# The setup of a graph layer's kernel in another order: list and first gathers before x, tables of chunk 0 before the lead groups

## The chip, the cores and the metric

The kernel runs on one core of a Trainium2 chip. The metric is the time of one execution on the device in microseconds (us), lower is better. The engines have short names in the profile: PE (TensorE, matmuls), PEld (its weight loads), DVE (VectorE), ACT (ScalarE), POOL (GpSimd) and SP (SyncE, which here only issues transfers); a q behind a name is that engine's instruction queue.

## The reference, cut to what matters

```python
def _L0_gnn_ref(x, edge_index, edge_attr, W1, b1, W2, b2, ln_w, ln_b, gn_w, gn_b, gn_ms):
    src, dst = (edge_index[0], edge_index[1])
    msg = x[src] + edge_attr
    agg = jax.ops.segment_sum(msg, dst, num_segments=N)
    h = jax.nn.relu(agg @ W1 + b1) @ W2 + b2
    ...   # a norm over all of h, a graph norm, gelu, + x
x = _layernorm(x + _L0_gnn_ref(x, edge_index, edge_attr_128, ...), axis=-1)
```

There are N = 6250 nodes with 128 features and E = 206250 edges, sorted by their target dst. For each node the kernel sums the 128 features of every incoming edge (edge_attr) and the features x of every edge's source node.

## The kernel before, in words

The aggregate agg (128 features x 6250 nodes, in SBUF) has two parts, and one long loop builds both.

*The edge part.* The edges are cut into 68 groups of 3072, and a group comes in two halves of 768 KB each, `edges`, in a ring of four slots (`HALVES = 4`). VectorE makes a one-hot matrix per half (`mark`, L1029), TensorE multiplies (`sum_half`, L722), ScalarE copies the sums (`copy_sums`, L573), TensorE puts them in place with a one-hot `place` (`turn_sums`, L736), and VectorE adds them to agg (`add`, L1053). The first four groups are the lead groups (`lead_groups`, `mark_lead`), halves 0 to 7; the rest run inside the chunk loop. A half's load waits until the half that had its slot has been read (semaphore `halves_free`); halves 8 to 12, which chunk 0 reads, wait for half 6, for half 7 (halves 9, 10 and 11) and for half 8.

*The source part.* The nodes are cut into 25 chunks of 250, that is 125 pairs. For each chunk TensorE counts how often each source node occurs: VectorE marks five batches (`mark_batch`, L1118, two bf16 comparisons each), TensorE counts 25 banks (`count_bank`, L774, 5 matmuls each), ScalarE copies each bank (`copy_bank`, L609), and then x is multiplied with the counts (L832, 98 matmuls, x split in two fp32r parts `x_hi` and `x_lo`). Banks 0 to 5 of a chunk are counted ahead, among the products of the chunk before. Chunk 0 has no chunk before it.

*What a chunk's marks need.* Each edge is one word with dst and src; the words are stored to a list in DRAM (`listed`). To find a pair's edges, two gathers by GpSimd follow each other for each chunk c: `begins(c)` (L479) reads 256 words around the pair's tile, VectorE counts the words below the pair and so finds the row (`stage_row`, L1076 to L1080), and `near(c)` (L486) reads the 128 words from there. VectorE splits the words (`split_words`, `widen_words`, `join_keys`, L1089 to L1103), TensorE turns them (`turn_keys`, L751), ScalarE copies them (`copy_keys`, L579), and the marks can start. `begins(c+1)` waits for `stage_tile(c+1)`, which stands behind `join_keys(c)` on VectorE. So the gathers of chunks 0, 1 and 2 are a chain through GpSimd, the DMA engines and VectorE.

*The setup.* SP loads dst, ACT loads src; VectorE packs the words (L982), ACT stores the list. A search finds for each pair the tile of 256 edges: three pieces, 7 sets each, marked by VectorE (piece 0, L962) or ScalarE (pieces 1 and 2, L553) and summed by TensorE (L694). In the kernel before, SP loads x as soon as src has landed, into the memory of the marks (`x_raw` in `pool_m`), so no mark can be written until x has been split. SP's queue is in order: dst, x, then the edge halves.

The order on each engine is written out by hand. The profile's lines are those of the functions below.

## Time and profile before

| | us |
|---|---|
| time, median of 3 runs (753.02 to 753.58) | 753.34 |
| the profiled execution | 756.05 |
| its span in the profile | 754.2 |

| engine | busy us | share of the span |
|---|---|---|
| PE | 691.8 | 92% |
| PEld | 628.4 | 83% |
| DVE | 631.5 | 84% |
| ACT | 424.5 | 56% |
| POOL | 115.1 | 15% |

The profiled execution takes 756.05 us, 1.85 us more than its span. The mean granted clock of TensorE is 0.974 of full speed. The page's first part gives busy time by engine; its second part cuts the span in 40 slices; its fourth part follows the work that ended last back from the end. A stretch can be asked for alone: the chain of waits in order of time, a timeline of instructions, or busy time by windows. Idle time of an engine matters only where somebody waits for it.

### The profile page before, as it was taken

What the parts mean: (1) busy time and instruction counts of PE and PEld (TensorE: products, weight loads), DVE (VectorE), ACT (ScalarE), POOL (GpSimd) and SP (SyncE); (2) the same over time, 40 slices, a digit from 0 to 9 for tenths busy, and PEclk for the clock granted to TensorE, in tenths of its full rate; (3) what the DMA queues carried; (4) which work ended last, traced back from release to release, by engine and by line L of the source; (5) the groups of instructions that cost most, each with busy time, mean ns of one, the idle gap of its engine ahead of it and who ended that gap; (6) DMA issues with size and microseconds to landing.
All of it is one profiled execution on the core that took longest, in us unless ns stands there. A gap on an engine that the chain in (4) does not pass through costs nothing.

```text
span 754.2 us, 25355 instructions
## 1 busy us (share of the span) xinstructions
PE 691.8 (92%) x9473; PEld 628.4 (83%) x9473; DVE 631.5 (84%) x1067; ACT 424.5 (56%) x962; POOL 115.1 (15%) x90
## 2 busy tenths in 40 slices
PE   0976899999999999999999999999999999999963
PEld 0965789988899888998899988999889998888842
DVE  4786989889899898998989989899898998835576
ACT  0943565466655666457564566646665466614447
POOL 2042301110011101111011110211101110100024
PEclk9995799999999999999999999999999999999996
DMA  6957535466354662556625665356553565400006
GB/s 136 329 191 220 182 99 198 152 219 209 88 190 170 214 209 71 196 185 212 196 74 187 206 208 172 100 179 217 189 172 119 177 219 172 144 16 0 0 1 170
DMA packets 87489, 120.41 MB, mean 160 GB/s; under 512 B 8718, under 2 KB 84486, under 8 KB 87267
## 3 DMA queue, kind: packets, MB, share of 16 engines
q1 hardware_dynamic: 80724, 113.10, 46.6%
q0 software_dynamic: 5744, 5.38, 2.7%
q10 hardware_dynamic: 1000, 1.65, 0.9%
q8 instruction: 13, 0.21, 0.1%
q14 instruction: 8, 0.07, 0.0%
HBM read 116.03 MB, written 4.03 MB: 159 GB/s over the span
## 4 chain that ended last, share of the span: by engine, by line
PE 76%; ACT 9%; DVE 5%; DMA 4%; issue 3%; POOL 1%; ACTq 0%; DVEq 0%; POOLq 0%; SPq 0%
PE bank L832 40%; PE bank L774 18%; PE bank L722 10%; ACT counts L609 6%; PE bank L876 3%; PE bank L866 3%; PE bank L736 2%; ACT below L553 2%; DMA begins<-listed,tile_slot 2%; DMA agg<-in_dst_dram 1%; DMA near<-listed,row_slot 1%; POOL pool_m L526 1%; DVE x_lo L1059 1%; PE bank L751 1%; DVE pool_m L1118 1%
## 5 line engine op out<-in xcount | busy, mean ns | idle before, releaser
L609 ACT CAST counts<-bank 128x490 fp32r<-128x490 f32 x600 | 320.1, 605 | 239.0 <-PE bank L774 236.1
L832 PE MATMUL bank<-counts,x_hi 128*128 128x250 f32 x1225 | 308.7, 291 | 8.5 <-ACT counts L609 8.4
L832 PE MATMUL bank<-counts,x_lo 128*128 128x250 f32 x1225 | 293.2, 279 | 0.0
L832 PEld LDWEIGHTS bank<-counts,x_hi 128*128 128x128 f32 x1225 | 231.1, 189 | 14.8 <-ACT counts L609 14.0
L1118 DVE TENSOR_TENSOR pool_m<-value_row,turned_lo 128x3328 bf16<-128x3328 bf16 (+1 forms) x125 | 229.1, 1833 | 12.1 <-PE bank L774 11.6
L832 PEld LDWEIGHTS bank<-counts,x_lo 128*128 128x128 f32 x1225 | 232.3, 190 | 0.0
L774 PE MATMUL bank<-pool_m 128*128 128x98 bf16 x3125 | 196.0, 211 | 8.6 <-DVE pool_m L1118 8.6
L774 PEld LDWEIGHTS bank<-pool_m 128*128 128x128 bf16 x3125 | 159.6, 99 | 28.3 <-issue 12.8
L1118 DVE TENSOR_TENSOR pool_m<-value_row,turned_key 128x2548 bf16<-128x2548 bf16 (+1 forms) x125 | 179.7, 1437 | 0.0
L486 POOL DMA_INDIRECT near<-listed,row_slot x27 | 53.6, 1986 | 501.6 <-DVE row_slot L1080 460.0
L722 PE MATMUL bank<-edges,onehot 128*32 128x128 f32 x3228 | 121.6, 284 | 5.9 <-DMA edges<-in_edge_attr_dram 3.9
L722 PEld LDWEIGHTS bank<-edges,onehot 128*32 128x32 f32 x3228 | 84.3, 112 | 18.6 <-issue 3.9
L1029 DVE TENSOR_TENSOR onehot<-value_row,dst_cols 128x384 f32<-128x384 bf16 x136 | 72.8, 553 | 0.0
L1053 DVE TENSOR_TENSOR agg<-agg,bank 128x128 f32 x68 | 19.4, 285 | 29.4 <-PE bank L736 27.9
L479 POOL DMA_INDIRECT begins<-listed,tile_slot x28 | 37.1, 1326 | 40.5 <-issue 29.7
L654 ACT ACTIVATE onehot<-bank,b1c 128x250 f32<-128x250 f32 x50 | 20.7, 465 | 27.3 <-PE bank L866 27.3
L573 ACT COPY sums<-bank 128x128 f32<-128x128 f32 x68 | 21.5, 316 | 22.3 <-PE bank L722 22.2
L736 PE MATMUL bank<-place,sums 128*128 128x128 f32 x136 | 32.3, 320 | 0.7 <-DVE place L1041 0.5
L736 PEld LDWEIGHTS bank<-place,sums 128*128 128x128 f32 x136 | 20.7, 191 | 11.8 <-issue 8.3
L1126 DVE CAST counts<-bank 128x490 fp32r<-128x490 f32 x25 | 16.6, 665 | 13.0 <-PE bank L774 13.0
L1331 DVE TENSOR_SCALAR agg<-bank,par 128x250 f32 x24 | 11.5, 478 | 17.3 <-PE bank L876 17.3
L866 PE MATMUL bank<-agg,pool_m 128*128 (+1 forms) x100 | 25.1, 374 | 0.8 <-DVEq L1315 0.8
(156 smaller groups left out, 461.7 us busy)
## 6 DMA issues: line engine op xcount, KB each, us to landing
edges<-in_edge_attr_dram SPq DMA_DIRECT2D x134, 768.0 KB
out_dram<-pool_m SPq DMA_DIRECT2D x12, 256.0 KB
agg<-in_dst_dram SPq DMA_DIRECT2D x1, 768.0 KB
agg<-in_src_dram ACTq DMA_DIRECT2D x1, 768.0 KB
listed<-agg ACTq DMA_DIRECT2D x1, 768.0 KB
begins<-listed,tile_slot POOLq DMA_INDIRECT x28, 4.2
near<-listed,row_slot POOLq DMA_INDIRECT x27
pool_m<-in_L_gnn_W_dram SPq DMA_DIRECT2D x2, 128.0 KB, 2.2
```

The lines of the kernel that those rows point to most:

```text
L479: pool.indirect_dma_start(begins[0:PAIRS, :], None, listed_rows, bass.IndirectOffsetOnAxis(tile_slot[0:PAIRS, 0:1], 0)).then_inc(begins_lo ...
L486: pool.indirect_dma_start(near[0:PAIRS, :], None, listed_rows, bass.IndirectOffsetOnAxis(row_slot[0:PAIRS, 0:1], 0)).then_inc(near_loaded, 16)
L573: nc.scalar.copy(sums[:, :], eps[s]).then_inc(sums_copied, 1)
L609: nc.scalar.copy(counts[:, :, at:at + NODES], cps[k % RING][:, 0:NODES * NT].rearrange("p (n q) -> p q n", q=NT)).then_inc(banks_free, 1)
L722: last = nc.tensor.matmul(eps[s][b * WINDOW:(b + 1) * WINDOW, :], oh[:, t, :], edges[:, u, t * D:(t + 1) * D], start=(k == 0 and j == 0), ...
L736: nc.tensor.matmul(turned_sum[s], sums[:, :], place[:, :], start=True, stop=True).then_inc(sums_turned, 1)
L774: last = nc.tensor.matmul(cps[k % RING][:, i * KEYS:(i + 1) * KEYS], mark_lo[b % MARKED][:, n // INTER, :, n % INTER], mark_key[b % MARKED ...
L832: last = nc.tensor.matmul(sps[:, 0:CHUNK], part[:, q, :], counts[:, q, at:at + CHUNK], start=(q == 0 and part is x_hi), stop=(q == NT - 1 ...
L866: last = nc.tensor.matmul(zps[u][:, k, 0:CHUNK], w1[:, k * P:(k + 1) * P], agg[:, bass.ds(c * CHUNK, CHUNK)], start=True, stop=True, skip_ ...
L876: last = nc.tensor.matmul(hps[u][:, 0:CHUNK], w2[:, k, :], hidden[:, u, k, :], start=(k == 0), stop=(k == HC - 1))
L1029: dve.tensor_tensor(oh, window, of.to_broadcast([P, HALF, WINDOW]), ALU.is_equal).then_inc(onehot_ready, 1)
L1118: last = dve.tensor_tensor(to[b % MARKED][:, 0:wide[1]], values[:, :, 0:n, :].to_broadcast(wide), of.to_broadcast(wide), ALU.is_equal)
```

## The change

Four things are put elsewhere; nothing is computed otherwise.

1. The small loads of dst and src (the last 3 full rows and the rest) are issued ahead of the large ones (64 rows). The padding of the last row no longer is a memset in the target: VectorE sets one row (`pad_row`), and GpSimd copies it with a DMA.
2. x is loaded into the place of `x_lo` (`x_in`) and split in place, so the memory of the marks is free. SP waits with x until `near(0)` has landed (`near_loaded`); the edge halves stand behind x in its queue.
3. `stage_row(0)` moves up, right behind `rows_ready`; `turn_keys(0)` stands inside the search's third piece, behind its fourth set; GpSimd issues `begins(1)` ahead of its memset of agg.
4. The marks and the first six banks of chunk 0 come before the lead groups, on VectorE, TensorE and ScalarE; the split of x stands behind the keys of chunk 1.

```diff
@@ -148,7 +148,9 @@
         below = nc.alloc_sbuf_tensor_at("below", [P, (len(PIECES) - 1) * SETS, SEARCH * PAIRS], BF16,
                                         offset=counts_at + (NPAIR + 7) // 16 * 32 + 32)
         x_hi = sb("x_hi", [P, NT, D], F32R)
+        x_lo_at = -(-nc.sbuf_base // 32) * 32
         x_lo = sb("x_lo", [P, NT, D], F32R)
+        x_in = nc.alloc_sbuf_tensor_at("x_in", [P, NT, D], F32, offset=x_lo_at)
         LW = P * BP
         KW = KEYS * BP
         pool_m = sb("pool_m", [P, max(2 * NT * D, MARKED * (LW + KW))], BF16)
@@ -376,15 +380,13 @@
         @block.sync
         def _(sp):
-            sp.dma_start(rows_i[0:EVEN, :], dst_full[0:EVEN, :]).then_inc(dst_loaded, 16)
-            sp.wait_ge(rows_padded, 2)
             sp.dma_start(rows_i[EVEN:FULL, :], dst_full[EVEN:FULL, :]).then_inc(dst_loaded, 16)
             sp.dma_start(rows_i[FULL:GROUPS, 0:REST], dst_rest).then_inc(dst_loaded, 16)
-            sp.wait_ge(src_loaded, 48)
+            sp.dma_start(rows_i[0:EVEN, :], dst_full[0:EVEN, :]).then_inc(dst_loaded, 16)
             sp.wait_ge(rows_padded, 3)
-            sp.dma_start(x_raw[:, 0:(NT - 1) * D].rearrange("p (t d) -> p t d", d=D),
-                         x[0:(NT - 1) * P, :].rearrange("(t p) d -> p t d", p=P)).then_inc(x_loaded, 16)
-            sp.dma_start(x_raw[0:LAST, (NT - 1) * D:NT * D], x[(NT - 1) * P:N, :]).then_inc(x_loaded, 16)
+            sp.wait_ge(near_loaded, 16)
+            sp.dma_start(x_in[:, 0:NT - 1, :], x[0:(NT - 1) * P, :].rearrange("(t p) d -> p t d", p=P)).then_inc(x_loaded, 16)
+            sp.dma_start(x_in[0:LAST, NT - 1, :], x[(NT - 1) * P:N, :]).then_inc(x_loaded, 16)
             def load(g, k, u, free):
                 sp.wait_ge(halves_free, free)
@@ -470,6 +472,8 @@
                 at, to = a * PAIRS, b * PAIRS if b < CHUNKS else NPAIR + 7
                 pool.iota(pair_row[:, at:to], [[1, to - at]], base=at, channel_multiplier=0,
                           allow_small_or_imprecise_dtypes=True).then_inc(pair_row_ready, 1)
+            pool.wait_ge(rows_padded, 2)
+            pool.dma_start(rows_i[FULL:GROUPS, REST:GROUP], pad_row).then_inc(pad_loaded, 16)
             for s, places in ((halves_free, HALVES), (sums_copied, 3), (sums_turned, 3), (edges_added, 2),
                               (banks_done, CREDIT), (chunk_summed, 1), (chunk_added, 1)):
                 pool.sem_inc(s, places)
@@ -491,12 +495,12 @@
             pool.wait_ge(consts_ready, 2)
             gather_begins(0)
             gather_near(0)
+            gather_begins(1)
             pool.wait_ge(turned, TURNS)
             pool.memset(agg[:, :], 0.0).then_inc(agg_zeroed, 1)
             with pool.Fori(1, CHUNKS + 2) as c:
-                gather_begins(c)
                 gather_near(c)
-            gather_begins(CHUNKS + 2)
+                gather_begins(c + 1)
             pool.wait_ge(begins_loaded, (CHUNKS + 3) * 16)
             pool.memset(ones, 1.0).then_inc(ones_ready, 1)
@@ -530,9 +534,9 @@
         @block.scalar
         def _(act):
-            act.dma_start(src_rows[0:EVEN, :], src_full[0:EVEN, :]).then_inc(src_loaded, 16)
             act.dma_start(src_rows[EVEN:FULL, :], src_full[EVEN:FULL, :]).then_inc(src_loaded, 16)
             act.dma_start(src_rows[FULL:GROUPS, 0:REST], src_rest).then_inc(src_loaded, 16)
+            act.dma_start(src_rows[0:EVEN, :], src_full[0:EVEN, :]).then_inc(src_loaded, 16)
...
@@ -561,12 +565,6 @@
                           ).then_inc(listed_stored, 16)
             search(1)
             search(2)
-            act.wait_ge(x_loaded, 32)
-            for i in range(NT // PIECE):
-                at = slice(i * PIECE, (i + 1) * PIECE)
-                nc.scalar.copy(x_hi[:, at, :], x_raw[:, i * PIECE * D:(i + 1) * PIECE * D].rearrange("p (t d) -> p t d", d=D)
-                               ).then_inc(x_high, 1)
-
             def copy_sums(g, s):
                 act.wait_ge(halves_free, g * 2 + (2 + HALVES))
                 act.wait_ge(sums_turned, g + 3)
@@ -621,8 +612,17 @@
                     if k == KEYS_COPY_AT and more:
                         copy_keys(c + 1)
+            act.wait_ge(pads_ready, 1)
+            copy_keys(0)
+            count_cover(0)
             for k in range(AHEAD):
                 copy_bank(0, k, 0)
+            act.wait_ge(x_loaded, 32)
+            for i in range(NT // PIECE):
+                at = slice(i * PIECE, (i + 1) * PIECE)
+                nc.scalar.copy(x_hi[:, at, :], x_in[:, at, :]).then_inc(x_high, 1)
+            for g in range(LEAD):
+                copy_sums(g, g % GPC)
             count_cover(1)
             with act.Fori(0, PAIRED) as p:
                 for odd in range(2):
@@ -751,11 +751,9 @@
                     last = nc.tensor.transpose(turn_ps[:, at:at + PAIRS], rows[0:PAIRS, :], ident[0:PAIRS, 0:PAIRS])
                 last.then_inc(keys_turned, 1)
-            search(2)
-            lead_groups(0)
+            search(2, range(SETS // 2 + 1))
             turn_keys(0)
-            lead_groups(GPC)
-            turn_sums(LEAD - 1, (LEAD - 1) % GPC)
+            search(2, range(SETS // 2 + 1, SETS))
             def count_bank(c, k):
@@ -833,9 +831,14 @@
                                                 start=(q == 0 and part is x_hi), stop=(q == NT - 1 and part is x_lo))
                 last.then_inc(chunk_summed, 1)
+            for k in range(COUNTED):
+                if k == RING - 1:
+                    pe.wait_ge(tiles_read, 2)
+                count_bank(0, k)
+            lead_groups(0)
+            lead_groups(GPC)
+            turn_sums(LEAD - 1, (LEAD - 1) % GPC)
             pe.wait_ge(x_split, NT // PIECE)
-            for k in range(COUNTED):
-                count_bank(0, k)
             with pe.Fori(0, PAIRED) as p:
                 for odd in range(2):
                     count_chunk(p * 2 + odd, p, odd, PER_PAIR)
@@ -939,10 +942,10 @@
             link(dve.memset(tile_end_i[:, :], 2 * N), setup, steps)
             dve.engine_nop().then_inc(rows_padded, 1)
-            link(dve.memset(rows_i[EVEN:96, REST:GROUP], PAD), setup, steps)
+            link(dve.memset(pad_row, PAD), setup, steps)
             dve.engine_nop().then_inc(rows_padded, 1)
             dve.memset(no_edges[:, :], NO_EDGE)
-            link(dve.memset(x_raw[96:P, (NT - 1) * D:NT * D], 0.0), setup, steps)
+            link(dve.memset(x_in[96:P, NT - 1, :], 0.0), setup, steps)
             dve.engine_nop().then_inc(rows_padded, 1)
             dve.wait_ge(consts_ready, 1)
             dve.tensor_scalar(pair_key[:, :], pair_i[:, :], -float(NT), None, ALU.mult)
@@ -1005,6 +1026,7 @@
             link(dve.tensor_copy(first_wide[0:GROUPS, :, :], first_gap[0:GROUPS, :].rearrange("g (s a) -> g s a", a=1)
                                  .to_broadcast([GROUPS, SUBS, WINDOW])), setup, steps)
             dve.engine_nop().then_inc(rows_ready, 1)
+            stage_row(0)
             dve.wait_ge(base_summed, 1)
             dve.tensor_copy(base_i[:, 0:GROUPS], sps[0:1, P:P + GROUPS])
@@ -1139,45 +1144,44 @@
                     at = agg[:, bass.ds(c * CHUNK, CHUNK)]
                     dve.tensor_tensor(at, at, sps[:, 0:CHUNK], ALU.add).then_inc(chunk_added, 1)
+            split_words(0)
+            widen_words(0)
+            join_keys(0)
+            stage_tile(1)
+            dve.wait_ge(pads_ready, 1)
+            mark_batch(0, 0)
+            dve.wait_ge(below_used, len(PIECES) * SETS)
+            read_tiles(PIECES[1][0], CHUNKS, signs=True)
+            dve.engine_nop().then_inc(tiles_read, 1)
+            mark_batch(0, 1)
+            stage_row(1)
             for g in range(GPC):
                 mark_lead(g, 0)
                 mark_lead(g, 1)
                 if g == 0:
                     put(g)
-            stage_row(0)
+            mark_batch(0, 2)
+            split_words(1)
+            widen_words(1)
+            join_keys(1)
+            stage_tile(2)
             for i in range(NT // PIECE):
                 split_x(i)
-            split_words(0)
-            widen_words(0)
-            join_keys(0)
-            stage_tile(1)
             dve.wait_ge(agg_zeroed, 1)
             for g in range(GPC, LEAD):
                 mark_lead(g, 0)
                 add(g - GPC, g % GPC, base_of(g - GPC))
                 put(g - 1)
                 mark_lead(g, 1)
-            dve.wait_ge(below_used, len(PIECES) * SETS)
-            read_tiles(PIECES[1][0], CHUNKS, signs=True)
-            dve.wait_ge(x_split, NT // PIECE)
-            dve.wait_ge(pads_ready, 1)
-            mark_batch(0, 0)
-            stage_row(1)
+            stage_row(2)
+            stage_tile(3)
+            mark_batch(0, 3)
             mark_pair(0, 0)
             add(LEAD - 2, 0, base_of(LEAD - 2))
             put(LEAD - 1)
             add(LEAD - 1, 1, base_of(LEAD - 1))
-            mark_batch(0, 1)
-            split_words(1)
-            widen_words(1)
-            join_keys(1)
-            stage_tile(2)
             mark_pair(0, 1)
             mark_pair(0, 2)
-            mark_batch(0, 2)
-            stage_row(2)
-            stage_tile(3)
-            mark_batch(0, 3)
             def even(c, p, last=False):
```

On VectorE before, from the one-hots of lead group 1 on: `begins` to `row_slot` is `stage_row(0)`, `x_lo` the split, `lo_i` to `node_i` the keys of chunk 0.

```order
L1029 TENSOR_TENSOR onehot<-value_row,dst_cols 128x384 x2
L1076 TENSOR_SCALAR begins,first_f<-begins,pair_w 125x256
L1078 SCALAR_TENSOR_TENSOR first_i<-tile_f,first_f 125x1
L1080 TENSOR_SCALAR row_slot<-first_i 125x1
L1059 TENSOR_TENSOR x_lo<-pool_m,x_hi 128x896 x7
L1089 TENSOR_SCALAR lo_i<-near 125x128
L1090 TENSOR_SCALAR node_i<-near 125x128
L1091 TENSOR_SCALAR near<-near 125x128
L1096 CAST lo_i<-lo_i 125x128
L1097 TENSOR_SCALAR node_i<-node_i,pair_key 125x128
L1103 TENSOR_TENSOR node_i<-node_i,near 125x128
L975 COPY tile_slot<-tile_rows 125x1
```

VectorE now, from the third batch of marks of chunk 0 (L1123) on; `near` here is that of chunk 1, and L1051 is the one-hot of lead group 2.

```order
L1123 TENSOR_TENSOR pool_m<-value_row,turned_lo 128x3328
L1123 TENSOR_TENSOR pool_m<-value_row,turned_key 128x2548
L1094 TENSOR_SCALAR lo_i<-near 125x128
L1095 TENSOR_SCALAR node_i<-near 125x128
L1096 TENSOR_SCALAR near<-near 125x128
L1101 CAST lo_i<-lo_i 125x128
L1102 TENSOR_SCALAR node_i<-node_i,pair_key 125x128
L1108 TENSOR_TENSOR node_i<-node_i,near 125x128
L978 COPY tile_slot<-tile_rows 125x1
L1081 TENSOR_TENSOR x_lo<-x_in,x_hi 128x896 x7
L1051 TENSOR_TENSOR onehot<-value_row,dst_cols 128x384
```

The split of x stood behind `stage_row(0)` and ahead of every key; it now stands behind the words of `near(1)` and ahead of the one-hots of lead groups 2 and 3.

On TensorE before, from the third piece of the search (L694) on; L722 are the edge halves, L774 the banks of chunk 0.

```order
L694 MATMUL bank<-ones_b,below 125x1 x77
L722 MATMUL bank<-edges,onehot 32x128 x36
L736 MATMUL bank<-place,sums 128x128
L722 MATMUL bank<-edges,onehot 32x128 x12
L751 MATMUL bank<-ident,lo_i 128x125
L751 MATMUL bank<-ident,node_i 128x125
L722 MATMUL bank<-edges,onehot 32x128 x12
L736 MATMUL bank<-place,sums 128x128
L722 MATMUL bank<-edges,onehot 32x128 x24
L736 MATMUL bank<-place,sums 128x128
L722 MATMUL bank<-edges,onehot 32x128 x12
```

TensorE now, from the same place; L772 are the banks.

```order
L694 MATMUL bank<-ones_b,below 125x1 x44
L751 MATMUL bank<-ident,lo_i 128x125
L751 MATMUL bank<-ident,node_i 128x125
L694 MATMUL bank<-ones_b,below 125x1 x33
L772 MATMUL bank<-pool_m 128x98 x30
L722 MATMUL bank<-edges,onehot 32x128 x36
L736 MATMUL bank<-place,sums 128x128
L722 MATMUL bank<-edges,onehot 32x128 x24
L736 MATMUL bank<-place,sums 128x128
L722 MATMUL bank<-edges,onehot 32x128 x24
```

The 30 matmuls of the first six banks now stand ahead of all edge halves, and the keys are turned between the fourth and the fifth set of the search.

## Rows read from the trace of the kernel before

**Rows 1.** Chain of waits from 86 us: start us, us, what

```profile
86.17 2.46 PE bank L832 x20
...
124.84 0.71 PE bank L774 x15
...
134.92 2.60 PE bank L832 x20
...
182.59 2.59 PE bank L832 x20
```

**Rows 2.** Stretches: us, busy us (count) of PE, PEld, DVE, ACT, POOL, clock, DMA share, GB/s

```profile
50.00:60.00 10.00, 5.60 (x104) 4.16 (x94) 7.07 (x17) 0.53 (x2) 1.50 (x2) 0.81 0.84 267
60.00:70.00 10.00, 5.37 (x71) 4.41 (x68) 6.99 (x13) 5.71 (x13) 1.65 (x1) 0.67 0.94 299
70.00:80.00 10.00, 6.32 (x85) 5.16 (x85) 7.58 (x12) 3.80 (x9) 4.39 (x3) 0.50 0.41 122
```

**Rows 3.** Chain of waits within the setup, columns as in rows 1

```profile
4.26 9.88 DMA agg<-in_dst_dram
...
49.07 7.64 DMA begins<-listed,tile_slot
...
58.52 7.44 DMA near<-listed,row_slot
...
68.35 5.55 DMA begins<-listed,tile_slot
```

**Rows 4.** Busy time of one quarter microsecond, columns as in rows 2

```profile
10.50:10.75 0.25, 0.00 (x0) 0.00 (x0) 0.00 (x0) 0.00 (x0) 0.00 (x0) 1.00 1.07 147
```

**Rows 5.** Timeline, VectorE: start us, us, engine line op out<-in xcount [idle before <-releaser]

```profile
14.23 3.42 DVE L982 SCALAR_TENSOR_TENSOR agg<-agg 68x426 int32<-68x426 int32 x2 [8.04 <-DMA agg<-in_dst_dram]
...
29.90 0.21 DVE L1005 COPY place<-first_gap 68x128 f32<-68x128 f32 x1
...
39.30 7.11 DVE L1059 TENSOR_TENSOR x_lo<-pool_m,x_hi 128x896 fp32r<-128x896 f32 x7 [0.57 <-ACT x_hi L567]
...
48.09 0.56 DVE L1029 TENSOR_TENSOR onehot<-value_row,dst_cols 128x384 f32<-128x384 bf16 x1
...
51.41 0.55 DVE L1029 TENSOR_TENSOR onehot<-value_row,dst_cols 128x384 f32<-128x384 bf16 x1
...
52.30 1.89 DVE L1118 TENSOR_TENSOR pool_m<-value_row,turned_lo 128x3328 bf16<-128x3328 bf16 x1
...
54.11 1.48 DVE L1118 TENSOR_TENSOR pool_m<-value_row,turned_key 128x2548 bf16<-128x2548 bf16 x1
```

**Rows 6.** Timeline, GpSimd, columns as in rows 5

```profile
39.66 1.81 POOL L486 DMA_INDIRECT near<-listed,row_slot  x1 [10.56 <-DVE row_slot L1080]
...
41.47 5.44 POOL L495 MEMSET agg<- 128x6378 f32 x1
...
58.52 1.21 POOL L486 DMA_INDIRECT near<-listed,row_slot  x1 [8.22 <-DVE row_slot L1080]
...
68.35 2.92 POOL L479 DMA_INDIRECT begins<-listed,tile_slot  x1 [8.63 <-DVE tile_slot L975]
```

**Rows 7.** Gathers begins (L479) from 90 to 640 us: issue to landing

```profile
DMA to landing us min/median/max: 3.5/4.1/5.4
```

**Rows 8.** Timeline, TensorE, columns as in rows 5

```profile
34.53 8.31 PE L694 MATMUL bank<-ones_b,below 128*125 128x1 bf16 x77
...
42.77 3.72 PE L722 MATMUL bank<-edges,onehot 128*32 128x128 f32 x72
...
52.34 0.86 PE L722 MATMUL bank<-edges,onehot 128*32 128x128 f32 x24 [1.47 <-DMA edges<-in_edge_attr_dram]
...
56.91 1.51 PE L722 MATMUL bank<-edges,onehot 128*32 128x128 f32 x24 [1.10 <-DMA edges<-in_edge_attr_dram]
...
58.92 0.77 PE L736 MATMUL bank<-place,sums 128*128 128x128 f32 x2 [0.50 <-DVE place L1041]
```

**Rows 9.** Timeline, SyncE's queue, columns as in rows 5

```profile
14.89 10.95 SPq L387 DMA_DIRECT2D pool_m<-in_x_dram  x1
```

41 lines of the change are left out of this document (19 added, 22 removed).

## The prediction

> **What bounds the kernel now.** I read the chain of waits first. From 86.17 us on it is TensorE that counts and multiplies: the product of chunk 0 starts at 86.17, that of chunk 2 at 134.92, that of chunk 4 at 182.59 [rows 1]. Two chunks take 47.67 us there, and the change touches nothing of them. So the time changes by as much as the product of chunk 0 starts earlier or later than 86.17, and all of the question lies ahead of it. There TensorE has little to do: it is busy for 5.6, 5.4 and 6.3 us of the three stretches of 10 us from 50 to 80, and its granted clock falls from full speed to half (the level of 1.2 GHz) [rows 2]. What ends the waits is the chain of gathers: begins(1) takes 7.64 us from issue to landing, near(1) 7.44, begins(2) 5.55 [rows 3]. Between them stands VectorE with x and the keys.
>
> **The parts, by one schedule.** I lay the new order out as one schedule in us of the span, from rows of before. Its end is compared with 86.17, and the difference added to the median of 753.34 (the profiled execution's own 756.05 lies 2.7 above that median, so only differences are carried over).
>
> *Loads of the list.* The last piece of dst lands at 14.14 [rows 3], and the small pieces are what comes late: their bytes still move at 10.50 to 10.75 [rows 4], behind the large ones. With the small ones first the same bytes go through the same few DMA engines in the other order, so I take only 0.8 us: 13.4. Bounds: 14.2 (nothing), and 11.6, if only the bytes' end at 10.7 and a short receipt count. The pad's DMA by GpSimd replaces a memset; nothing waits for it before the list has landed, and at most 5.4 us of flight, as for a small gather [rows 7], hide in that. If it landed after 13.4, everything would shift with it.
>
> *List to row_slot(0).* VectorE starts to pack at 14.23 and ends the last table of the rows at 30.11 [rows 5]: 15.9 us, unchanged, so 29.3. The list's store starts 0.8 earlier and without x in front of it; begins(0), issued at 27.5 before, lands by 29 at the latest I can see, under the same tables. stage_row and GpSimd's reaction: begins(1) landed at 56.71 and near(1) was issued at 58.52 [rows 3], 1.8 us. So near(0) is issued at 31.1, before 39.66 [rows 6]. The DMA engines are idle now, and a gather then lands after 4.1 us [rows 7]: 35.1. That is what the reordering gains, 8.6 us on near(0).
>
> *Behind near(0).* near(1) landed at 65.96 and begins(2) was issued at 68.35 [rows 3]: keys, tile and reaction take 2.4 us. So begins(1) is issued at 37.6. But x was issued at 35.1 by the same event, and begins(1) now flies beside x: 7.6 us as in rows 3, landing at 45.3 (4.1 us and 41.7 as the lower bound). TensorE reaches the fourth set of the search's third piece 0.7 earlier than before: 33.8 plus four of seven sets of 8.31 us [rows 8], 38.6; turn and copy about 0.9; the marks start at 39.5. Two batches at 3.3 and 3.1 us [rows 5] with 0.4 for the tiles: 46.4. So stage_row(1) waits for VectorE, not for the gather, and near(1) is issued at 46.4 + 1.8 = 48.2. GpSimd's memset of agg, 5.44 us [rows 6] from 38.9, ends at 44.4 and hides.
>
> *near(1) meets the edge halves.* SP is held 10.95 us by x's issue [rows 9], so the halves start at 47, just ahead of near(1). I take the flight of before beside halves, 7.44 [rows 3]: 55.6. VectorE marks lead groups 0 and 1 (2.2 us) and the third batch (3.4) until 52.9 and then waits 2.7 us. The split of x is now queued behind that wait, and behind the split the one-hots of lead groups 2 and 3.
>
> *From near(1) to half 6.* Keys and tile 1.5, split of x 7.11 [rows 5]: 64.2. One-hot, add, place: 0.9, so TensorE reads half 4 from 65.1; halves 4, 5 and 6 and one turn at the low clock take 3 x 1.51 and 0.77 [rows 8]: 70.4. Before, half 7 began at 56.91 already.
>
> *What is late next: the halves of chunk 0.* Half 8's load waits for half 6, halves 9 to 11 for half 7, half 12 for half 8. In before half 0 was read by 43.6 (42.77 plus a quarter of the 3.72 us for three halves with a gap), and four halves later TensorE, waiting for each, began half 7 at 56.91 [rows 8]: 13.3 us for four, and 2.3 for one more (52.34 to 56.91 are two). So half 12 lands at 70.4 + 13.3 + 2.3 = 86.0; its 12 matmuls 0.9 and a turn 0.8 give 87.7.
>
> *VectorE's and the banks' own way* ends earlier. Lead groups 2 and 3 take 3.9 us (48.09 to 51.96) [rows 5]: 68.1; stage_row(2) and the tile 1.0, fourth batch 3.1, one-hot, add and place 1.2: 73.4; turn_sums(3) 0.8 [rows 8]: 74.2. From there 19 banks and five halves take 10.1 us where all is ready (124.84 to 134.92) [rows 1]: 84.3. Before, that stretch took 26.5 us from 59.7, waiting for marks. So nearly all that marks cost before is saved, and given back because VectorE and the halves start late.
>
> The sum: 87.7 against 86.2, +1.5 us, so 754.9.
>
> **Two rules.** What the row shows: near(1) and begins(1) took 7.44 and 7.64 us beside halves, 4.1 where little else moves [rows 3, 7]. The Trainium skill (DMA: Bandwidth & Descriptors, "Queues, rings and completion order") says that each DMA engine goes round robin between its queues packet by packet, by which a gather would hardly be held up; the trace speaks against that, but the rival below gets a chance for it. The other rule bears on GpSimd. A gather took 2.92 us on GpSimd beside a mark and 1.21 without one, while the memset ran 5.44 us beside the split of x [rows 6]. The Trainium skill (SBUF — State Buffer, "Who interferes with whom") has a VectorE instruction with two SBUF inputs hold up a GpSimd instruction that reads SBUF, not one that only writes; the trace agrees with both halves, and it is why I give the memset no price.
>
> **Rivals.** *Gathers fly free* (faster than the forecast): x's and the halves' packets don't hold them. near(1) lands at 52.3 and VectorE is bound by its third batch, 52.9: 2.7 us less, so 85.0, -1.2: 752.1. Against it are both rows of 3. *The other side, clearly faster:* the same, and the list lands at 11.6, as its bytes suggest. Everything behind shifts by another 1.8: 83.2, -3.0: 750.4. It decides from the point where near(1) lands before 51. With contended gathers and the list at 11.6 it is 85.9: 753.1, within no change. *Marks block gathers:* begins(1) or near(1) is issued beside a mark and waits 1.7 us (2.92 less 1.21), and once it is late, VectorE waits at stage_row(1) too: +1.7 to +3, so 757.2. For it: batches stand close to both issues. *The clock stays low:* TensorE idles from 45 to 52 and sparsely to 64, and is still at half speed while it counts chunk 0. A half's matmuls then take 1.51 us instead of 0.86 [rows 8], 3.3 us over five halves, partly under the waits for the loads: +1.4, 756.3. *Wrong place:* x is not needed before the first product, so the split could be free; but it stands ahead of the lead groups, and so it is not.
>
> **How the numbers follow.** The forecast's case has 0.38 (754.9, and 753.9 to 756.4 with it), free gathers 0.14, clearly faster 0.10, early list 0.12, blocked gathers 0.14, low clock 0.12. A difference below 0.2%, 1.5 us, can't be told from none. Of the forecast's case a little more than half lies above 754.85, of the blocked and slow-clock cases nearly all, so slower 0.46; free gathers and clearly faster give 0.20 of faster with a part of the early list; same 0.34. The bounds (list 11.6 to 14.2, flight 4.1 to 7.6, blocks of 1.7 twice) reach from 750.4 to 758.3; I take 751.2 to 758.0.
>
> **What would show it.** In the profile of the changed kernel: dst landing near 13.4; near(0) issued at 31; marks of chunk 0 from 39.5; near(1) landing at 55.6 with VectorE idle before `lo_i`; the split of x ending at 64; half 12 as the last thing ahead of the first product, at 87.7, and that product's rhythm of 47.67 us as before. The forecast is wrong if near(1) lands before 53, if the halves stream in so early that TensorE never waits for one after 75, or if the first product starts before 85.

## The result

| | us |
|---|---|
| before, median of 5 runs | 753.34 (751.97 to 754.02) |
| after, median of 5 runs | 757.90 (756.66 to 758.99) |
| ratio after to before | 1.0062, 95% interval 1.0045 to 1.0079 |
| profiled execution after: time, span | 756.66, 754.8 |

The change makes the kernel slower by some 4.6 us; 1.5 were forecast. The time lies inside the range, but the difference is three times the forecast one.

The profiled execution is the fastest of the five. The chain of waits of the kernel after (start us, us, what) holds what answers to [rows 1, 3]:

```profile
5.42 7.90 DMA agg<-pool_m
13.52 3.44 DVE agg L1003 x2
...
49.55 6.50 DMA near<-listed,row_slot
...
77.13 9.11 DMA edges<-in_edge_attr_dram
87.59 2.59 PE bank L830 x20
...
135.66 2.59 PE bank L830 x20
...
183.31 2.59 PE bank L830 x20
```

The product of chunk 0 starts at 87.59, where 87.7 was forecast and [rows 1] had 86.17; ahead of it stands the load of half 12, as forecast. It is no clear bound, though: TensorE, without a wait since half 10, ends the 20 matmuls ahead of half 12 (from 85.05, 1.10 us) only 0.1 us before that half lands at 86.24. Two chunks further it is 135.66 against 134.92, then 183.31 against 182.59: the later rhythm takes 0.7 us back, and from there 47.65 us for two chunks is what it was.

GpSimd's and SyncE's timelines after, which answer to [rows 6, 9] (start us, us, engine line op, tiles, idle before and its releaser):

```profile
31.03 1.21 POOL L490 DMA_INDIRECT near<-listed,row_slot  x1 [5.36 <-DVE row_slot L994]
38.11 1.20 POOL L483 DMA_INDIRECT begins<-listed,tile_slot  x1 [5.88 <-DVE tile_slot L978]
39.31 5.44 POOL L500 MEMSET agg<- 128x6378 f32 x1
49.55 1.21 POOL L490 DMA_INDIRECT near<-listed,row_slot  x1 [4.81 <-DVE row_slot L994]
```

```profile
35.02 8.86 SPq L389 DMA_DIRECT2D x_in<-in_x_dram  x1
43.92 43.80 SPq L393 DMA_DIRECT2D edges<-in_edge_attr_dram  x17
```

near(0) goes out 8.6 us earlier than in [rows 6]. What that costs stands in the second fence: the edge halves, whose loads began at 25.9 before (14.89 + 10.95, [rows 9]), now begin at 43.92.

VectorE's timeline after, answering to [rows 5]:

```profile
56.08 0.23 DVE L1094 TENSOR_SCALAR lo_i<-near 125x128 int32<-125x128 int32 x1 [2.14 <-DMA near<-listed,row_slot]
...
57.47 7.12 DVE L1081 TENSOR_TENSOR x_lo<-x_in,x_hi 128x896 fp32r<-128x896 f32 x7
```

It waits 2.14 us for near(1) and then splits x for 7.12, while TensorE's timeline, answering to [rows 8], shows who needs VectorE in that time:

```profile
65.35 1.51 PE L722 MATMUL bank<-edges,onehot 128*32 128x128 f32 x24 [4.78 <-DVE agg L1075]
...
67.52 2.72 PE L722 MATMUL bank<-edges,onehot 128*32 128x128 f32 x48
...
75.41 1.51 PE L722 MATMUL bank<-edges,onehot 128*32 128x128 f32 x24
...
78.28 0.86 PE L722 MATMUL bank<-edges,onehot 128*32 128x128 f32 x24 [0.31 <-DMA edges<-in_edge_attr_dram]
...
82.06 0.86 PE L722 MATMUL bank<-edges,onehot 128*32 128x128 f32 x24 [1.63 <-DMA edges<-in_edge_attr_dram]
...
86.28 0.86 PE L722 MATMUL bank<-edges,onehot 128*32 128x128 f32 x24
```

These are half 4, halves 5 and 6, half 8, half 9, half 10, half 12. Half 4 waits 4.78 us for VectorE; half 8's load waits for half 6, which ends at 70.24. The stretches show the hole that this leaves in the transfers (columns as in [rows 2]):

```profile
63.00:66.00 3.00, 0.65 (x13) 0.68 (x17) 3.00 (x7) 0.00 (x0) 0.00 (x0) 1.00 1.07 270
66.00:69.00 3.00, 3.00 (x48) 2.30 (x42) 1.66 (x6) 0.00 (x0) 0.00 (x0) 1.00 0.23 78
69.00:72.00 3.00, 2.45 (x54) 1.69 (x43) 2.93 (x7) 0.75 (x3) 1.64 (x1) 1.00 0.14 13
72.00:75.00 3.00, 1.51 (x14) 1.48 (x15) 1.95 (x6) 0.81 (x4) 1.71 (x2) 0.74 0.98 324
```

### The profile page after: what moved, and what is told of

Read it like the earlier page. It is cut to its first block, busy times and chain, and to the rows that moved or that the text cites. A ratio compares the mean times of both kernels' runs of the same rounds, so it can differ in the third digit from the quotient of the medians.

```text
span 754.8 us, 25382 instructions
## 1 busy us (share of the span) xinstructions
PE 691.8 (92%) x9473; PEld 627.8 (83%) x9473; DVE 631.0 (84%) x1067; ACT 424.3 (56%) x962; POOL 117.5 (16%) x91
## 4 chain that ended last, share of the span: by engine, by line
PE 79%; ACT 7%; DVE 5%; DMA 3%; issue 3%; POOL 2%; ACTq 1%; DVEq 0%; POOLq 0%; SPq 0%
PE bank L830 40%; PE bank L772 17%; PE bank L722 10%; ACT counts L600 6%; PE bank L879 3%; PE bank L869 3%; PE bank L736 3%; PE bank L694 2%; DVE pool_m L1123 1%; DMA edges<-in_edge_attr_dram 1%; DMA agg<-pool_m 1%; POOL pool_m L530 1%; PE bank L751 1%; DMA near<-listed,row_slot 1%; DVE x_lo L1081 1%
## 5 line engine op out<-in xcount | busy, mean ns | idle before, releaser
L1123 DVE TENSOR_TENSOR pool_m<-value_row,turned_lo 128x3328 bf16<-128x3328 bf16 (+1 forms) x125 | 229.1, 1832 | 15.4 <-PE bank L772 11.9
L772 PE MATMUL bank<-pool_m 128*128 128x98 bf16 x3125 | 193.7, 210 | 2.8 <-DVE pool_m L1123 2.8
L1123 DVE TENSOR_TENSOR pool_m<-value_row,turned_key 128x2548 bf16<-128x2548 bf16 (+1 forms) x125 | 179.6, 1437 | 0.0
L772 PEld LDWEIGHTS bank<-pool_m 128*128 128x128 bf16 x3125 | 157.5, 98 | 21.9 <-issue 5.5
L722 PE MATMUL bank<-edges,onehot 128*32 128x128 f32 x3228 | 122.4, 285 | 12.4 <-DMA edges<-in_edge_attr_dram 7.3
L722 PEld LDWEIGHTS bank<-edges,onehot 128*32 128x32 f32 x3228 | 84.6, 113 | 26.0 <-issue 7.7
L1051 DVE TENSOR_TENSOR onehot<-value_row,dst_cols 128x384 f32<-128x384 bf16 x136 | 72.7, 552 | 0.0
L483 POOL DMA_INDIRECT begins<-listed,tile_slot x28 | 39.4, 1407 | 39.3 <-issue 25.8
L1075 DVE TENSOR_TENSOR agg<-agg,bank 128x128 f32 x68 | 19.3, 284 | 31.1 <-PE bank L736 30.3
L736 PEld LDWEIGHTS bank<-place,sums 128*128 128x128 f32 x136 | 20.9, 193 | 13.4 <-issue 10.9
```

Of the source, the lines that this page charges most:

```text
L483: pool.indirect_dma_start(begins[0:PAIRS, :], None, listed_rows, bass.IndirectOffsetOnAxis(tile_slot[0:PAIRS, 0:1], 0)).then_inc(begins_lo ...
L722: last = nc.tensor.matmul(eps[s][b * WINDOW:(b + 1) * WINDOW, :], oh[:, t, :], edges[:, u, t * D:(t + 1) * D], start=(k == 0 and j == 0), ...
L736: nc.tensor.matmul(turned_sum[s], sums[:, :], place[:, :], start=True, stop=True).then_inc(sums_turned, 1)
L772: last = nc.tensor.matmul(cps[k % RING][:, i * KEYS:(i + 1) * KEYS], mark_lo[b % MARKED][:, n // INTER, :, n % INTER], mark_key[b % MARKED ...
L1051: dve.tensor_tensor(oh, window, of.to_broadcast([P, HALF, WINDOW]), ALU.is_equal).then_inc(onehot_ready, 1)
L1123: last = dve.tensor_tensor(to[b % MARKED][:, 0:wide[1]], values[:, :, 0:n, :].to_broadcast(wide), of.to_broadcast(wide), ALU.is_equal)
```

## The experiments

Ratios are those to the kernel before, run beside it on the same chip, with 95% intervals; 0.0013 is one microsecond. A ratio can differ by up to 0.0014 from the quotient of the two medians (for warm by 0.0018). In all traces the span less the start of the product of chunk 0 is 666.2 to 668.2 us, so a span tells within 2 us where that product stood. Batches of marks are counted from 0, as in `mark_batch(0, 3)`.

### The kernel before again (c_before)

No edit.

> The kernel before once more, for a second trace of it beside its timed runs. Theory A (the one profiled execution of it was not typical): the median of its runs is again near 753.3, the span 751.5, and the product of chunk 0 starts between 83 and 84.5, not at 86.17; what differs is the landing of the gathers and halves ahead of 86. Rival B (the profiler itself costs 2.7 us in this kernel): the span is again 754.2 and the product starts at 86.2 +- 0.3, while the timed runs stay at 753.3.

Measured: ratio 0.9995 (0.9982 to 1.0007), and in the trace the product of chunk 0 starts at 84.27. The spans of 40 executions of the kernel before on this chip lie between 749.6 and 753.3, median 751.7. The profiled execution on which the forecast rests had 754.2, and of 63 later ones on three other chips one has more (754.4): it was not typical. Theory A holds. TensorE's timeline in the new trace:

```profile
57.42 1.51 PE L722 MATMUL bank<-edges,onehot 128*32 128x128 f32 x24 [1.04 <-DMA edges<-in_edge_attr_dram]
...
69.13 0.87 PE L774 MATMUL bank<-pool_m 128*128 128x98 bf16 x15 [1.81 <-DVE pool_m L1118]
...
76.63 0.99 PE L774 MATMUL bank<-pool_m 128*128 128x98 bf16 x10 [5.01 <-DVE pool_m L1118]
...
84.27 0.38 PE L832 MATMUL bank<-counts,x_hi 128*128 128x250 f32 x1
```

and VectorE's:

```profile
63.41 0.22 DVE L1089 TENSOR_SCALAR lo_i<-near 125x128 int32<-125x128 int32 x1
```

Half 7 is read at 57.42, later than in [rows 8] (56.91), and yet the product comes 1.9 us earlier. In this trace VectorE takes the words of near(1) at 63.41, straight behind its marks, where near(1) landed at 65.96 in [rows 3]; all behind it is earlier. The gather itself took 4.1 us from 58.02, not 7.44 from 58.52, although edge halves move beside it in both: 277 GB/s here, 311 there.

### The kernel after again (c_after)

No edit.

> The changed kernel once more, for a second trace and more timed runs. Its trace so far was that of the fastest of its five runs (span 754.8, the others 755.0 to 757.2). Theory 1 (the product of chunk 0 alone carries the time; the rest from its start to the end of the span is 667.3 +- 0.6 in all traces): median 757 to 758 again, product at span less 667.3, with the whole difference ahead of it. Theory 2 (TensorE's low clock is what differs between its runs): where the span is above 756, half 8 or banks behind it run at half clock for longer than the 1.5 us seen in the first trace. Rival: the gathers' landings differ, near(1) lands 1 us or more later than 56.05.

Measured: 756.87 us, ratio 1.0057 (1.0038 to 1.0075); spans 753.7 to 756.9. With the five runs above the median span of 11 is 755.8, which is 4.1 above the 751.7 of before. The new trace has just this span, and its product starts at 89.04. near(1) landed after 6.6 us against 6.5 in the first trace, so the rival is out. What differs comes from 78 us on. The stretches of the second trace:

```profile
78.00:81.00 3.00, 1.03 (x24) 0.86 (x24) 2.41 (x3) 0.64 (x2) 0.00 (x0) 0.88 1.06 309
81.00:84.00 3.00, 3.00 (x48) 2.60 (x45) 0.50 (x3) 1.69 (x5) 0.00 (x0) 0.55 1.05 355
```

The first trace was at full speed in both. TensorE's timeline shows what was at work there:

```profile
79.97 1.29 PE L722 MATMUL bank<-edges,onehot 128*32 128x128 f32 x24 [2.51 <-DMA edges<-in_edge_attr_dram]
...
81.66 1.84 PE L772 MATMUL bank<-pool_m 128*128 128x98 bf16 x20
...
89.04 0.38 PE L830 MATMUL bank<-counts,x_hi 128*128 128x250 f32 x1 [0.27 <-ACT counts L600]
```

Two things come together. Half 9 is read 1.7 us later than in the first trace, although half 4 was 0.7 earlier: TensorE waited 2.51 us for its transfer, and why that was slower stays open. And the work from half 9 to half 10 then takes 3.46 us instead of 2.15 (20 of its matmuls 1.84 us instead of 1.09). In the first trace TensorE stood idle for 1.63 us ahead of half 10, which would nearly have taken up either of the two alone. Together they give 1.7 + 1.3 - 1.6, the 1.4 us by which the product is later. Theory 2 holds for this pair in so far as the low clock is needed, but it isn't alone.

Of these six runs the three at a mean clock of 0.989 had spans of 753.7 to 754.3, the three at 0.980 to 0.982 spans of 755.8 to 756.9. This is weak evidence: the first five runs are less orderly (0.983 had 755.0, 0.984 had 757.1), and some two thirds of the difference in mean clock between the two traces lie from 63 to 72, where halves 4 to 7 took nearly the same time in both (see the last section).

### The first part alone (loads_only)

The kernel before, with the new order of the six loads of dst and src, and the pad by GpSimd's DMA.

```diff
-            sp.wait_ge(rows_padded, 2)
+            pool.wait_ge(rows_padded, 2)
+            pool.dma_start(rows_i[FULL:GROUPS, REST:GROUP], pad_row).then_inc(pad_loaded, 16)
```

> The kernel before with only the first part of the change: the small pieces of dst and src are issued ahead of the large ones, the large piece no longer waits for the memset, and GpSimd loads the pad by a DMA. Forecast's term: the list lands 0.8 us earlier (13.3 to 13.4), all behind it moves by as much, time 0.5 to 1 us below the kernel before. Rival: the pad's DMA is the last to land and takes back the gain, time within 0.3 us. Other rival: x, issued behind src, now meets the store of the list more fully, begins(0) and near(0) are later by up to 1 us, time 0 to 1 us above.

Measured: ratio 1.0007 (0.9994 to 1.0019): nothing. In the trace VectorE starts to pack at 13.06, 1.1 us earlier than the 14.15 of c_before, and near(0) goes out at 38.66 instead of 39.59; the pad's DMA is the last to land, as the first rival has it. The 0.8 us of the forecast are there at the front. The product starts at 83.64 in this trace, 0.6 us before that of c_before, and the timed runs show nothing that stands out of the noise.

### x early (x_early)

```diff
-            sp.wait_ge(near_loaded, 16)
+            sp.wait_ge(src_loaded, 48)
             sp.dma_start(x_in[:, 0:NT - 1, :], ...).then_inc(x_loaded, 16)
             sp.dma_start(x_in[0:LAST, NT - 1, :], ...).then_inc(x_loaded, 16)
+            sp.wait_ge(near_loaded, 16)
```

> The changed kernel with x loaded as early as before (behind the list's loads, ahead of the store), and only the edge halves waiting for near(0). Theory 1 (the forecast's: the split of x in front of lead groups 2 and 3 sets when half 4 is read, and that sets half 12): half 4 is still read at 64 to 65, half 12 still lands near 86, time within 1 us of the changed kernel's 757.9. Rival 2 (the late start of the edge halves, issued at 44 instead of 26, is what costs): the halves are issued near 35, half 12 lands 3 to 5 us earlier, time 753 to 755. Rival 3 (the store and begins(0) are held up by x's bytes): near(0) is issued 1 to 3 us later than 31.0 and the time rises to 759 to 760.

Measured: 755.17 us, ratio 1.0022 (1.0014 to 1.0031), so 0.0035 to 0.0040 or 2.6 to 3 us better than the kernel after. Half 4 is read at 62.97 and the product starts at 85.84. Rivals 2 and 3 both come true in part: the halves are issued at 35.57, near(0) at 32.34 instead of 31.03, and the first outweighs the second; the time lies 0.2 us above rival 2's interval, and half 12 is read only 1.9 us earlier (84.34). near(1) now flies while little else moves (89 GB/s against 356), and lands after 3.9 us instead of 6.5. VectorE's and TensorE's timelines:

```profile
53.71 0.22 DVE L1095 TENSOR_SCALAR lo_i<-near 125x128 int32<-125x128 int32 x1
...
55.09 7.12 DVE L1082 TENSOR_TENSOR x_lo<-x_in,x_hi 128x896 fp32r<-128x896 f32 x7
```

```profile
55.47 0.86 PE L723 MATMUL bank<-edges,onehot 128*32 128x128 f32 x24
62.97 1.51 PE L723 MATMUL bank<-edges,onehot 128*32 128x128 f32 x24 [6.64 <-DVE onehot L1052]
```

Halves 0 to 3 are done at 56.3, and TensorE waits 6.64 us for the split of x to pass: theory 1's wait is there too, and larger. So the earlier halves don't help half 4 by themselves. They are through when near(1) flies, the split starts 2.4 us earlier (55.09 instead of 57.47), and half 4 is read 2.4 us earlier.

### The split of x elsewhere (split_last, spread, early_mid)

split_last moves the split behind the last one-hot of the setup:

```diff
-            for i in range(NT // PIECE):
-                split_x(i)
             dve.wait_ge(agg_zeroed, 1)
...
             mark_pair(0, 2)
+            for i in range(NT // PIECE):
+                split_x(i)
```

> The changed kernel with the split of x on VectorE moved from ahead of lead groups 2 and 3 to behind the last one-hot of the setup (TensorE waits for it at the product of chunk 0 and no longer ahead of bank 6). Theory 1: the first add ends near 58.5, half 4 is read at 59 instead of 65.35, half 12 lands at 80 to 81, VectorE's fourth and fifth batch come 3 to 5 us earlier, and the product of chunk 0 starts at 81 to 83.5: time 752 to 754, 4 to 6 below the changed kernel. Rival 2 (the edge halves are late by their own issue and bandwidth, whatever VectorE does): half 12 lands within 1.5 us of 86 again, time 756.5 to 758.

Measured: 756.74 us, ratio 1.0046 (1.0032 to 1.0061). Half 4 is read at 60.10 and half 6 at 64.91, but half 12 only at 84.58 and the product starts at 85.74. TensorE's timeline says why:

```profile
60.10 1.51 PE L722 MATMUL bank<-edges,onehot 128*32 128x128 f32 x24 [0.54 <-DMA edges<-in_edge_attr_dram]
...
75.87 0.86 PE L722 MATMUL bank<-edges,onehot 128*32 128x128 f32 x24 [2.42 <-DMA edges<-in_edge_attr_dram]
...
82.75 0.86 PE L722 MATMUL bank<-edges,onehot 128*32 128x128 f32 x24
...
84.58 0.86 PE L722 MATMUL bank<-edges,onehot 128*32 128x128 f32 x24
```

These are half 4, half 9, half 11 and half 12. Halves 4 and 9 no longer wait for VectorE but for their transfer, and half 11 stands behind banks whose marks VectorE makes only after the split, at 79.01: the wait left half 4 and came back at batch 4. By its numbers rival 2 holds (half 12 within 1.5 us of 86, 756.74 us), but its reason only in part. The trace is of the fastest of the six runs, 1.9 us below their median.

spread lays the seven pieces into VectorE's idle times: two ahead of `split_words(1)`, one behind the first one-hot of group 2, three behind the first of group 3, one behind the last.

> The changed kernel with VectorE's split of x laid into its idle times: two pieces of seven while it waits for near(1), one behind the first one-hot of group 2, three behind the first of group 3, one behind the last. Theory 1 (half 8's load waits until half 6 is read, and half 6 waits for VectorE): half 4 is read at 60, half 6 by 66.5, half 12 lands by 82, batch 4 comes by 76, and the product of chunk 0 starts at 82 to 83.5: time 751 to 753, about 5 below the changed kernel and at or below the kernel before. Rival (DMA bandwidth alone: 13 halves and x at 290 to 375 GB/s behind a start at 44): half 12 is still the last, at 85 or later, time 755 or more.

Measured: 754.08 us, ratio 1.0010 (0.9997 to 1.0023), 3.5 us better than the kernel after, product at 85.58. Half 4 is read at 61.46, half 6 at 66.34, half 12 at 84.04. The direction of theory 1 holds and its size not. Of the 2 us that it missed, 0.7 are the 20 matmuls behind half 9 that again ran at 1.84 us; ahead of half 9 TensorE waited 1.92 us for the transfer.

early_mid is x_early with the split between the one-hots of groups 2 and 3 and `stage_row(2)`.

> The changed kernel with x loaded as early as before, and the split of x behind lead groups 2 and 3 instead of ahead of them. x early alone gave 755.2. Theory 1: with halves 0 to 3 read by 55, half 4 is read at 56 to 57 instead of 62.97 and half 6 by 60; half 8's load starts 6 us earlier, TensorE no longer waits for halves 8 to 12, and 19 banks and five halves take some 10.5 us from 71 to 72: product at 82 to 83, time 751 to 752.5. Rival (VectorE is the bound there, since all its work from 55 to batch 4 is the same): batch 4 ends at 76.7 as with x early alone and the product starts at 84.5 to 86, time 754 to 755.5.

Measured: 754.47 us, ratio 1.0016 (1.0003 to 1.0028), product at 84.99. Half 6 was read by 64.2, yet the rival holds: TensorE stood idle for 5.96 us ahead of 72.28, for the place of group 3, which VectorE makes behind the split and batch 3. So with x early, moving the split alone changed nothing that stands out of the noise (1.0022 and 1.0016).

### TensorE kept busy (warm, busy_bf16)

Both add matmuls to the kernel after, in three waits: ahead of half 0, ahead of half 4, ahead of the turn of group 3. warm takes 50, 70 and 30 of this kind:

```diff
+                    nc.tensor.matmul(sps[:, 0:WINDOW], ident[:, :], ident[:, 0:WINDOW], start=True, stop=True,
+                                     skip_group_check=True)
```

> The changed kernel with TensorE kept busy by matmuls of a constant into the idle bank of the product, in three of its waits: 50 ahead of half 0, 70 ahead of half 4, 30 ahead of the turn of group 3. They add to no result. Theory 'clock' (halves 0 to 6 at 1.51 us instead of 0.86, and half 8, cost time, and make the runs differ): matmuls of a half take 0.86 throughout, half 6 is read some 1.5 us earlier, product 1 to 2 us earlier and the runs lie within 1 us of each other: time 755.5 to 757. Rival: the clock falls as before; the extra matmuls run on into the time in which halves could be read: 0 to +1.5 us.

Measured: 795.24 us, ratio 1.0576. Each such fp32 matmul stands in the trace as two records (100 for the 50), and these take 21.5 us ahead of half 0, some 0.2 us a record; the run tells nothing of the waits. It shows one thing of the clock, in its stretches:

```profile
50.00:60.00 10.00, 10.00 (x48) 10.00 (x49) 7.83 (x14) 5.06 (x7) 1.34 (x2) 1.00 0.71 236
...
80.00:90.00 10.00, 10.00 (x49) 10.00 (x48) 0.00 (x0) 0.00 (x0) 0.00 (x0) 0.50 0.11 39
```

The row reads half speed in a stretch in which TensorE is busy throughout. It reads full speed from 50 to 60, and yet as many of these matmuls are done there (48 against 49).

busy_bf16 takes 35, 40 and 15 matmuls of the marks' kind:

```diff
+                    nc.tensor.matmul(sps[:, 0:KEYS], mark_lo[1][:, 0, :, 0], mark_key[1][:, 0, :, 0], start=True,
+                                     stop=True, skip_group_check=True)
```

> The changed kernel with TensorE kept busy in the same three waits by matmuls of the marks' own kind (20 of them took 1.11 us at full clock): 35 ahead of half 0 (1.9 us), 40 ahead of half 4 (2.2), 15 ahead of the turn of group 3 (0.8), into the product's idle bank; they add to no result. The fp32 ones before took 0.2 us each, 38 us in all, and said nothing. Theory 'clock': more of the halves take 0.86 instead of 1.51 us, half 6 is read up to 1.5 us earlier, the banks behind half 8 run at 1.11, and the median falls by 1 to 2 us to 755.5 to 756.5. Rival: the clock falls as before and nothing moves by more than 0.5 us: 757 to 758.

Measured: ratio 1.0016 (1.0002 to 1.0030), 3 us better than the kernel after with work added and nothing taken away. TensorE's timeline:

```profile
60.33 2.04 PE L750 MATMUL bank<-pool_m 128*128 128x98 bf16 x40
64.93 0.86 PE L722 MATMUL bank<-edges,onehot 128*32 128x128 f32 x24 [2.56 <-DVE onehot L1059]
...
66.14 1.52 PE L722 MATMUL bank<-edges,onehot 128*32 128x128 f32 x48
...
86.77 0.39 PE L835 MATMUL bank<-counts,x_hi 128*128 128x250 f32 x1
```

Half 4 takes 0.86 us instead of 1.51, halves 5 and 6 take 1.52 instead of 2.72, and half 6 is done at 67.7 instead of 70.2. The clock theory holds, and the gain is larger than the 1 to 2 us it named. It comes from halves 4, 5, 6 and 8 and the banks ahead of half 8, which all run at full speed now. The 35 matmuls ahead of half 0 changed nothing, halves 0 to 3 take 1.5 us each as before; and half 10 waits 2.24 us for its transfer, with 20 matmuls at 1.84 us behind it. Two of its 12 spans, 755.7 and 757.9, still lie high.

### Where it points (early_order, halves_first, early_busy)

early_order is x_early with VectorE's order changed once more (the lines taken away are left out):

```diff
+            mark_lead(2, 0)
+            add(0, 0, base_of(0))
+            put(1)
+            mark_lead(2, 1)
+            mark_lead(3, 0)
+            for i in range(3):
+                split_x(i)
+            add(1, 1, base_of(1))
+            put(2)
+            mark_lead(3, 1)
+            for i in range(3, 5):
+                split_x(i)
+            add(LEAD - 2, 0, base_of(LEAD - 2))
+            put(LEAD - 1)
+            mark_pair(0, 0)
             stage_row(2)
             stage_tile(3)
             mark_batch(0, 3)
             add(LEAD - 1, 1, base_of(LEAD - 1))
             mark_pair(0, 1)
             mark_pair(0, 2)
+            for i in range(5, NT // PIECE):
+                split_x(i)
```

ScalarE rounds x in two stretches between its copies of the sums, and TensorE waits for the split at the product.

> The changed kernel with x loaded early; VectorE makes the one-hots of groups 2 and 3 before the split of x, lays three pieces of the split and then two between the adds, does the place of group 3 and half 8's one-hot ahead of stage_row(2), and the last two pieces behind the third of the pair's one-hots; ScalarE rounds x between copies of the sums; TensorE waits for the split only at the product. With x early and the split merely behind the one-hots, TensorE stood idle for 5.96 us (66.3 to 72.28) for the place of group 3. Theory 1 (that order in front of bank 6 is what is left): the turn of group 3 comes at 66 to 67, banks 6 to 16 are counted behind it while VectorE still marks, batch 4 ends by 77.5 and the product starts at 80 to 81.5: time 748.5 to 751, below the kernel before. Rival (VectorE's work is the bound, and low clock eats the rest): product at 83 to 84.5, time 752 to 753.5.

Measured: 749.63 us against 754.26, ratio 0.9948 (0.9935 to 0.9961): by the ratio 3.9 us better than the kernel before and some 7 better than the kernel after (1.0057 to 0.9948). The product starts at 79.40, in TensorE's timeline:

```profile
56.56 0.86 PE L729 MATMUL bank<-edges,onehot 128*32 128x128 f32 x24 [1.75 <-DVE agg L1082]
...
65.40 0.86 PE L779 MATMUL bank<-pool_m 128*128 128x98 bf16 x15
...
78.36 0.86 PE L729 MATMUL bank<-edges,onehot 128*32 128x128 f32 x24
...
79.40 0.36 PE L838 MATMUL bank<-counts,x_hi 128*128 128x250 f32 x1
```

Half 4 is read at 56.56, bank 6 counted from 65.40 (74.05 in the kernel after), half 12 read at 78.36. Theory 1 holds; the product is even 0.6 us ahead of its interval. How much of this is the place of the split and how much the rest of the order was not taken apart.

halves_first loads halves 0 to 3 behind near(0), and x behind them.

> As the kernel with x early and the new order, but the first four edge halves are loaded behind near(0) and x behind them, so that nothing of x stands beside the list's store and the first two gathers. Theory 1 (what matters is that the halves come early; x has time until the product): near(0) is issued at 31.0 instead of 32.3, halves 0 to 3 are read from 48.5 on, x lands near 52, product within 1 us of that of the other kernel, time 748.5 to 751. Rival (near(1) flies beside x and lands at 56 again, and the split starts late): product 1.5 to 3 us later than there, time 751.5 to 753.5.

Measured: ratio 1.0003 (0.9992 to 1.0014), 4 us behind early_order. Half 0 is read at 48.43 and half 4 only at 60.97, after 6.86 us of waiting for its transfer, which stands behind x; the product starts at 84.38, 5 us after that of early_order, where the rival had 1.5 to 3. The rival holds and is larger than priced: near(1), beside x, is taken at 56.40, and x fills the very time in which halves 4 to 7 have to come.

early_busy adds 24 matmuls of the marks' kind ahead of half 4 and 24 ahead of half 6 to early_order.

> The kernel of early_order (749.63, 0.9948 of the kernel before) with 24 matmuls of the marks' kind ahead of half 4 and 24 ahead of half 6, where TensorE waited 1.75 and 2.26 us for VectorE's adds; they add to no result. In the trace without them half 6, 7 and 8 took 1.39, 1.44 and 1.51 us and 20 matmuls of banks 1.70. Theory 'clock' (three such stretches gave the changed kernel about 2.7 us): the halves and banks run at 0.86 and 1.11, product of chunk 0 at 78 to 79 instead of 79.40, ratio to the kernel before 0.992 to 0.9945. Rival: DMA of halves 11 and 12, at 375 GB/s and saturated from 66 on, holds the product at 79 to 79.6 whatever the clock: ratio 0.9945 to 0.996.

Measured: 750.17 us, ratio 0.9959 (0.9946 to 0.9971): nothing gained. Its trace is of a run 2 us above its median; the product starts at 84.02, outside both forecasts. TensorE's timeline:

```profile
60.06 1.51 PE L729 MATMUL bank<-edges,onehot 128*32 128x128 f32 x24 [2.48 <-DMA edges<-in_edge_attr_dram]
61.50 2.14 PE L759 MATMUL bank<-pool_m 128*128 128x98 bf16 x24
63.58 1.51 PE L729 MATMUL bank<-edges,onehot 128*32 128x128 f32 x24
```

Half 5 waits 2.48 us for its transfer, the 24 matmuls behind it run at half speed for 2.14 us, and half 6 is read at 63.58 instead of 60.90. Halves 9, 11 and 12 wait for transfers too (0.47, 0.59 and 1.54 us). The rival holds as far as the time goes. But in this trace the added matmuls neither kept the clock up nor stayed out of the way, so it does not show that the clock would give nothing here.

## Why the prediction was wrong

By its own steps, against the first trace of the kernel after:

- *Loads of the list*: forecast 13.4, landed 13.32. The last to land is the pad's DMA (7.90 us, forecast at most 5.4); in the other traces with it VectorE packs the list from 12.72 to 13.82, here from 13.52.
- *near(0) at 31.1, landing 35.1*: 31.03, and it landed after 3.0 us.
- *begins(1) at 37.6, 7.6 us of flight*: 38.11 and 8.7; hidden as forecast, since VectorE came to stage_row(1) at 47.79.
- *Marks from 39.5, near(1) at 48.2, landing 55.6*: 40.43, 49.55, 56.05.
- *The edge halves start at 47*: 43.92, 3.1 us early; hidden, since half 4 waits for VectorE.
- *The split ends 64.2, half 4 at 65.1, half 6 done 70.4*: 64.59, 65.35, 70.24.
- *Half 12 lands 86.0, product at 87.7*: 86.24 and 87.59.

So the mechanism and its schedule stand, and spread shows that what the forecast named as the cause, the split ahead of half 4, does cost time. What failed is the last step, which reads "Its end is compared with 86.17, and the difference added to the median". The 2.7 us between the profiled execution and the median were taken for an offset that both kernels share. They were not: in that one execution the setup itself was late (near(1), [rows 3]), and the product at 86.17 is where a long run of the kernel before has it. In a run near the median it starts at 84.27. The schedule took durations from the late run (near(1)'s 7.44 us, measured 6.50), but came out at 87.7, near the 87.59 of one of the shorter runs of after. So its end should have been set against 84.3, which gives 3.4 us, or against the profiled run's own 756.05, which gives 757.6.

The rest bears on a rival that was given 0.12, *the clock stays low*, priced at +1.4. Between the two traces of after the product moves by 89.04 - 87.59, 1.45 us, and that took both the low clock behind half 9 (1.3 us) and the later transfer of half 9 (1.7 us), less the wait of 1.63 us that they used up. That the size is the rival's is in part luck. The sum is 1.42 (87.59 - 86.17) + 1.90 (86.17 - 84.27) + 1.45 = 4.77, and the spans of the two later traces differ by 4.7 (755.8 - 751.1); median against median it is 4.1. (86.17 is read from the chain of waits; by TensorE's timeline, as 84.27 is, it is 86.05.)

By parts of the change, in ratios: the loads 1.0007, which is nothing; with the tables in front, near(0) early and x in its own place 1.0022; with x moved behind near(0) as well 1.0057 and 1.0062. So 2.6 to 3 of the 4 us come from x's load, which holds the edge halves back from 35.57 to 43.92. The way goes through the forecast's own chain: held back, the halves meet near(1), its words come at 56.08 instead of 53.71, and the split and half 4 follow. What makes the remaining 1.7 us of x_early was not taken apart.

*Gathers fly free* is refuted for the changed kernel: near(1), issued 49.4 to 49.6 in after and x_early, takes 6.5 us beside the halves and 3.9 us where they are through. The Trainium skill (DMA: Bandwidth & Descriptors, "Queues, rings and completion order") says that each DMA engine goes round robin between its queues, switching at packets. From this the forecast took that a gather would hardly be held up, and this pair does not bear it out. In the order of before it isn't refuted: near(1) took 7.44 us in the first trace, but 4.1 in c_before and 3.6 in loads_only, with the halves moving beside it (277 GB/s in both flights). *Marks block gathers* did not come: both issues took 1.20 and 1.21 us. *Wrong place*, x's split in front of the lead groups, was right: laying it into idle times was worth 3.5 us (spread). With x early the move alone was worth 0.5 us, which is within the noise (early_mid), and together with the rest of early_order 5.6.

## What to carry to other kernels

A profile is one draw. Before its schedule is compared with a median, look whether its own time is a typical one, and build forecast and base in the same way; here the base was 1.9 us off, and on the way that ends at half 12 no time of the schedule more than 1.4. Where a chain of small gathers is brought forward, ask what bulk load is held back for it, and which later gather that load will then meet: an order on one queue moves everything that stands behind. Work that nobody needs soon belongs into the idle times of its engine in small pieces, not in front of what others wait for.
